# Routing of a two-block early-fusion network: the search for each expert's threshold, the ranking and the index rebuilt

## The reference

```
probs = softmax(x @ router_gate)                 # 3072 tokens, 8 experts
topw, topi = top_k(probs, 2);  topw /= topw.sum + 1e-9
gates[token, expert] = topw where chosen, else 0
top_g, tok_idx = top_k(gates.T, cap)             # cap = 960 tokens an expert
xe = x[tok_idx]
ye = (silu(xe @ gate_w) * (xe @ up_w)) @ down_w * top_g
out[tok_idx] += ye
```

## Time and profile before

| | |
|---|---|
| median of 3 runs | 2027.98 us (2025.38 to 2030.83) |
| profiled execution | 2033.92 us, its span 2032.1 us |
| PE, DVE, ACT, POOL busy | 1774.8, 1245.7, 973.9, 542.5 us |
| mean granted TensorE clock | 0.932 of full |
| PE in the chain that ended last | 70% |

### The profile page before, as it was taken

How to read it: one execution, slowest core, us unless ns; L and a number is a source line. 1 busy time by engine, 2 the same in 40 slices (tenths; PEclk the granted TensorE clock), 3 DMA queues, 4 the chain that set the end, 5 groups by cost and what they waited for, 6 DMA issues and landing times.

```text
span 2032.1 us, 35703 instructions
## 1 busy us (share of the span) xinstructions
PE 1774.8 (87%) x10949; PEld 1411.1 (69%) x10949; DVE 1245.7 (61%) x4049; ACT 973.9 (48%) x2658; POOL 542.5 (27%) x784
## 2 busy tenths in 40 slices
PE   3457999999999999899999999971369999999997
PEld 2245676767677676667777777751259989999896
DVE  6346686767768575856767677646745454445442
ACT  2025474665657566564666656630034353434431
POOL 2143334242433411111111111110052335333431
PEclk9568899999999999999999999985579999999999
DMA  6110101101010110102001110011032212212210
GB/s 188 48 34 17 50 2 57 34 24 58 0 42 0 55 32 1 32 1 79 6 31 31 31 31 23 16 61 29 0 119 90 81 47 95 76 53 69 73 38 20
DMA packets 74572, 90.20 MB, mean 44 GB/s; under 512 B 16539, under 2 KB 64710, under 8 KB 74472
## 3 DMA queue, kind: packets, MB, share of 16 engines
q1 hardware_dynamic: 65000, 72.32, 11.1%
q0 software_dynamic: 9472, 16.77, 2.9%
HBM read 71.09 MB, written 25.26 MB: 47 GB/s over the span
## 4 chain that ended last, share of the span: by engine, by line
PE 70%; issue 12%; DVE 8%; POOL 3%; DMA 2%; ACT 1%; DVEq 1%; POOLq 1%; SPq 1%; ACTq 0%
PE bank L1020 16%; PE bank L1490 16%; PE bank L1505 9%; PE bank L968 6%; PE bank L952 5%; PE bank L1003 5%; PE bank L891 2%; PE bank L1162 2%; PE bank L979 1%; PE bank L1042 1%; PE bank L876 1%; DVE probs L2120 1%; PE bank L892 1%; POOL rstd_a L2849 1%; PE bank L1475 1%
## 5 line engine op out<-in xcount | busy, mean ns | idle before, releaser
L1608 ACT ACTIVATE probs<-probs,nmax 128x128 f32<-128x128 f32 (+2 forms) x768 | 381.0, 501 | 75.0 <-DVE nmax L2120 74.8
L968 PE MATMUL bank<-cst,probs 128*128 128x128 f32 x1536 | 234.9, 279 | 19.5 <-ACT probsT L1616 11.8
L968 PEld LDWEIGHTS bank<-cst,probs 128*128 128x128 f32 x1536 | 182.8, 143 | 67.8 <-issue 25.4
L1490 PE MATMUL bank<-xeT,gate_w 128*128 128x480 f32 x768 | 187.1, 379 | 1.5 <-DVEq L2788 1.5
L1490 PE MATMUL bank<-xeT,up_w 128*128 128x480 f32 x768 | 186.9, 379 | 0.0
L2215 DVE COPY probsT<-bank 128x384 f32<-128x384 f32 x256 | 141.2, 552 | 72.1 <-PE bank L968 70.4
L1505 PE MATMUL bank<-down_w,hT 128*120 128x256 f32 x1536 | 182.8, 281 | 0.0
L1505 PEld LDWEIGHTS bank<-down_w,hT 128*120 128x120 f32 x1536 | 181.5, 182 | 0.1
L1616 ACT COPY probsT<-bank 128x384 f32<-128x384 f32 x256 | 121.9, 476 | 115.6 <-PE bank L968 107.0
L2891 POOL COPY rinv<-rowsum 128x384 f32<-128x384 f32 x80 | 40.8, 510 | 497.1 <-DVE o1T L2142 294.5
L2796 DVE TENSOR_TENSOR prod<-bank,sil 128x480 f32<-128x480 f32 x128 | 83.5, 656 | 146.3 <-PE bank L1490 146.3
(11 more groups left out here) (300 smaller groups left out, 3362.9 us busy)
## 6 DMA issues: line engine op xcount, KB each, us to landing
gate_raw<-in_L_ffn_gate_w SPq DMA_DIRECT2D x8, 1024.0 KB, 4.9
up_raw<-in_L_ffn_up_w SPq DMA_DIRECT2D x8, 1024.0 KB, 6.9
down_raw<-in_L_ffn_down_w SPq DMA_DIRECT2D x8, 1024.0 KB
img<-in_x SPq DMA_DIRECT2D x8, 768.0 KB, 5.5
residual_rows<-x SPq DMA_DIRECT2D x8, 384.0 KB, 2.5
residual_rows<-h_in SPq DMA_DIRECT2D x8, 384.0 KB, 3.8
xr<-residual_rows SPq DMA_DIRECT2D x8, 384.0 KB, 4.7
hr<-residual_rows SPq DMA_DIRECT2D x8, 384.0 KB, 3.9
```

The costliest lines, as they stand in the source:

```text
L968: last = tr(ps[bank][:, P * q:P * (q + 1)], probs[:, n % 4, SEG[t] + P * j:SEG[t] + P * (j + 1)], ident)
L1490: last = mm(ps[bank][:, 0:HALF], w[:, wp, c, P * m:P * (m + 1)], xeT[:, xp, c, HALF * hf:HALF * (hf + 1)], start=(c == 0 and k == 0), stop ...
L1608: last = f(p, p, ACT.Exp, bias=nmax[:, n % 4, t:t + 1], scale=-1.0, accum_out=rowsum[:, where, t:t + 1])
```

## The change

It has these parts:

1. **Output projection.** PE waits for the division of the pair before the last, sums seven of the eight products of each of the three tiles (in banks 0, 1 and 2, which stay open), and only then makes the last pair's values and turned divisors. The eighth products follow when the last pair is divided.
2. **Search on turned gates.** The gates of one expert (24 columns) are cut into two halves of 12; PE turns the two halves, so that 96 partitions (8 experts by 12) hold 256 tokens each. A candidate is then one number for each partition. A round is three scalar operations with an accumulated count, a product with a 96 x 96 matrix of "same expert", and four or five small operations. Its 15 rounds are written out, with the bits as constants. The threshold is turned back by PE.
3. **One ranking pass.** Ties and clear winners are summed, scanned and ranked in one pass of 384 columns.
4. **Index for expert 0 alone.** Its places are made from expert 0's column by itself (24 one-hot groups in three operations, 24 products), and its gather starts with `first_index`. The index for the others is made in the time of expert 0: one-hots on DVE (`others_hot`) before `hidden`, products on PE after the third pair of sums, the copy on DVE at the third step of `hidden`. Expert 0 is taken out of the loops of PE and DVE for that. The gather of expert 1 waits for this index.
5. **Weight split of expert 0.** ACT no longer waits for the index, and the lower part of the gate and up weights is made by POOL instead of DVE, before its wait for the index.

The core of the diff:

```
+            def rows_out(chunks):
+                for t in range(NT):
+                    ...
+                    for c in chunks:
+                        last = mm(ps[bank][:, 0:D], o1T[:, c, P * t:P * (t + 1)], wo1[:, c, :],
+                                  start=(c == 0), stop=(c == PAIRS - 1))
+            pe.wait_ge(freed[5], take0[5] + 2 * B + PAIRS * B - 1)
+            rows_out(range(PAIRS - 1))
             heads_out(1, PAIRS - 1, last_u)
             denominators_transposed(EPI, 0, "rinvT_tail", 1, last_u, PAIRS - 1)
             pe.wait_ge(freed[5], take0[5] + 2 * B + PAIRS * B)
-            for t in range(NT):
-                token_major(EPI, 0, "proj1", t, o1T, wo1, 8)
+            rows_out((PAIRS - 1,))
...
+            for r in range(SEARCH):
+                pe.wait_ge(counts_ready, r + 1)
+                mm(ps[7][0:GROUPS, 0:STEPS], const_cols("same_expert")[0:GROUPS, :], cnt[:], start=True, stop=True)
...
+            for name, left in (("totals", "ones"), ("earlier", "before")):
+                mm(ps[bank][:, 0:2 * E * TILES], const_cols(left), sel_eq[:].rearrange("p k n -> p (k n)"), ...
...
+            for n in range(TILES):
+                last = mm(ps[bank][0:CP, 0:CT], first_row[:, n, :], first_col[:, n, :], ...
...
+                    if q == 3 and aside is not None:
+                        aside()                      # PE: the 48 index products
...
+            gates(EXPERT, 0, 0, other_slots)
+            rows_transposed(EXPERT, 1, 0)
+            down(EXPERT, 0, 0)
+            with pe.Fori(1, E - 1) as e:
...
-            act.wait_ge(index_ready, 1)
             gate_uppers(0)
...
+            for r in range(SEARCH):
+                for q in range(STEPS):
+                    last = ts(at_least[:, q, :], by_group[:], as_gate[:, q:q + 1], 0.0, ALU.is_ge, ALU.add,
+                              accum_out=cnt[:, q:q + 1])
+                last.then_inc(counts_ready, 1)
+                if r > 0:
+                    tt(thr[:], thr[:], best[:], ALU.bitwise_or)
+                if r + 1 < SEARCH:
+                    then()
+                    tt(ahead[:], thr[:].to_broadcast([GROUPS, STEPS]), bits[:, r + 1, :], ALU.bitwise_or)
+                dve.wait_ge(counts_taken, r + 1)
+                stt(won[:], ps[7][0:GROUPS, 0:STEPS], float(CAP), bits[:, r, :], ALU.is_ge, ALU.mult)
+                then()
+                v.tensor_reduce(best[:], won[:], AX.X, ALU.max)
+                then()
+                if r + 1 < SEARCH:
+                    tt(cand[:], ahead[:], best[:].to_broadcast([GROUPS, STEPS]), ALU.bitwise_or)
...
+            v.tensor_copy(both(scan), k[:, 0:2 * E * TILES])
+            v.tensor_tensor_scan(both(earlier), const_cols("scan_keep"), both(scan), 0.0, ALU.mult, ALU.add)
...
+            tt(first_col[:], places(TILES, CT), spread(first_f[:, 1, :], CT), ALU.is_equal)
+            tt(first_row[:], places(TILES, CP), spread(first_f[:, 0, :], CP), ALU.is_equal)
+            tt(first_col[:], first_col[:].bitcast(F32), spread(token, CT), ALU.mult).then_inc(first_hot, 1)
...
+            def others_hot(g):
+                q, n = 8 * g, 8 * g % TILES
+                tt(col_hot[:, q:q + 8, :], places(8, E * CT), spread(col_f[:, q:q + 8], E * CT), ALU.is_equal)
+                tt(row_hot[:, q:q + 8, :], places(8, CP), spread(row_f[:, q:q + 8], CP), ALU.is_equal)
+                then()
+                tt(col_hot[:, q:q + 8, :], col_hot[:, q:q + 8, :].bitcast(F32), spread(token[:, n:n + 8], E * CT),
+                   ALU.mult).then_inc(hot_ready, 1)
...
-            gate_lowers(0)
             x_lowers(ROUTE, 0, 0)
+            for g in range(2 * TILES // 8):
+                others_hot(g)
+            down_lowers(0)
+            hidden(EXPERT, 0, 0, other_slots)
...
+            pool.wait_ge(gate_upper, 1)
+            for w, raw in ((gate_w, gate_raw), (up_w, up_raw)):
+                last = g.tensor_tensor(w[:, 1].rearrange("p c n -> p (c n)"), raw[:],
+                                       w[:, 0].rearrange("p c n -> p (c n)").bitcast(F32), ALU.subtract)
+            last.then_inc(gate_split, 1)
             pool.wait_ge(rows_cleared, 1)
             pool.wait_ge(gates_stored, 16)
-            pool.wait_ge(index_ready, 1)
+            pool.wait_ge(first_index, 1)
```

More of the change, by code:

```diff
@@ L472, in early_fusion_kernel @@
         (hT,), _ = region(end_e, ("hT", [P, 2, FM, CAP], F32R))
[L474 to L482, removed]
+        (pr, hots, gts, r_a, r_b, r_c), end_r = region(
+            end_e, ("pr", [P, E, TILES], F32), ("hots", [P, 2, E, TILES], F32),
+            *[(n, [P, E, TILES], F32) for n in ("gts", "r_a", "r_b", "r_c")])
@@ L1449, in _ @@
[L1449 to L1458, removed]
-            for q in range(2 * TILES):
-                if q % 8 == 0:
-                    pe.wait_ge(hot_ready, q // 8 + 1)
-                last = mm(ps[bank][0:CP, 0:E * CT], row_hot[:, q, :], col_hot[:, q, :],
-                          start=(q == 0), stop=(q == 2 * TILES - 1))
@@ L1464, in _ @@
-            last.then_inc(filled[bank], 1)
+                mm(ps[bank][:, 0:2 * E * TILES], const_cols(left), sel_eq[:].rearrange("p k n -> p (k n)"),
+                   start=True, stop=True).then_inc(filled[bank], 1)
+            pe.wait_ge(first_hot, 1)
+            bank = banks.bank(ROUTE, "first_index")
+            banks.wait_free(pe, ROUTE, "first_index")
+            for n in range(TILES):
+                last = mm(ps[bank][0:CP, 0:CT], first_row[:, n, :], first_col[:, n, :],
+                          start=(n == 0), stop=(n == TILES - 1))
@@ new lines, in _, with other_slots @@
+            last.then_inc(filled[bank], 1)
+            def other_slots():
+                bank = banks.bank(ROUTE, "index")
+                banks.wait_free(pe, ROUTE, "index")
+                for q in range(2 * TILES):
+                    if q % 8 == 0:
+                        pe.wait_ge(hot_ready, q // 8 + 1)
+                    last = mm(ps[bank][0:CP, 0:E * CT], row_hot[:, q, :], col_hot[:, q, :],
+                              start=(q == 0), stop=(q == 2 * TILES - 1))
+                last.then_inc(filled[bank], 1)
@@ L2719, in _ @@
             then()
-            tt(r_c[:], r_c[:], want[:].unsqueeze(2).to_broadcast([P, E, TILES]), ALU.is_lt)
+            k, f_ = bank_of(ROUTE, "earlier")
+            tt(both(earlier), both(scan), k[:, 0:2 * E * TILES], ALU.add).then_inc(f_, 1)
             then()
-            tt(r_c[:], r_c[:], eqm[:], ALU.mult)
+            ties_before, above_before = (earlier[:, z, :].rearrange("p (e n) -> p e n", e=E) for z in range(2))
+            left = want[:].unsqueeze(2).to_broadcast([P, E, TILES])
@@ L2729, in _ @@
             then()
[L2730 to L2741 removed]
+            stt(flat(r_c), flat(r_b), -float(NO_SLOT), flat(r_a), ALU.add, ALU.mult)
@@ new lines, in _ @@
+            tt(hot_code[:].rearrange("p k e n -> p k (e n)"), hots[:].rearrange("p k e n -> p k (e n)"),
+               flat(r_b).unsqueeze(1).to_broadcast([P, 2, E * TILES]), ALU.mult)
+            k, f_ = bank_of(ROUTE, "first_index")
+            ts(slot_token[0:CP, 0:CT], k[0:CP, 0:CT], float(NO_TOKEN), None, ALU.add).then_inc(f_, 1)
+            then()
+            v.nop().then_inc(first_index, 1)
+            for k in range(2):
+                v.tensor_reduce(kv[:, 6 + k, :], hot_code[:, k].rearrange("p e n -> p n e"), AX.X, ALU.add)
@@ L2742, in _ @@
+            then()
+            ts(code[:], kv[:, 6:8, :].rearrange("p k n -> p (k n)"), float(NO_SLOT), None, ALU.add)
             then()
@@ L2789, in x_lowers, with hidden @@
                 v.nop().then_inc(x_split, 2 * DC)
-            def hidden(section, e, i):
+            def hidden(section, e, i, aside=None):
                 for q in range(2 * FM + 1):
+                    if q == 2 and aside is not None:
+                        aside()
                     if q < 2 * FM:
```

199 lines of the change are left out of this document (107 added, 92 removed).

## The result

The changed kernel took 2008.17 us (median, 2007.8 to 2010.69) against 2029.4 for the kernel before in the same comparison: a ratio of 0.9896, interval 0.9871 to 0.9922, so 21.2 us less. 2010 was forecast, 17.7 us less. Run again later it gave 2011.81 against 2029.41, ratio 0.9917 (0.9901 to 0.9932). Its profiled execution took 2010.69, span 2008.9.

A forecast was written before the change was run, and what follows sets the result against it. A 149.2 us chain of dependent steps from the last attention values to expert 0's first product was taken as the bound. +1.8 +0.3 -9.7 +1.0 +6.5 -21.0 -5.6 +9.0 = -17.7 us gave a 2010 us median, range 1997 to 2021.

The forecast's parts named there:

- Projection, +1.8: Output projection: 21 of 24 products early fill no idle gap and queue DVE's three tiles; 1.8 us later, bounds 0 and +3.
- Search, -8.7 with fetches: Threshold search: fifteen rounds of 2.8 us gain 9.7, less 1.0 guessed for fetches of unrolled code.
- POOL's split, +6.5 (way in +0.3): Search's start: POOL's weight split holds DVE's two-input SBUF operations, 6.5 us; extra steps before the first scan, 0.3.
- From the last threshold to the gather, -21.0: Ranking and expert 0's index: 42.2 us become 21.2, bounds 18 and 25.
- The gather, -5.6: First gather to expert 0's first product: 21.4 us become 15.8, without DVE's split and expert 1's weights beside it.
- The alternative of -14.8 in all: Expert 0's gather: by the skill page DVE's two-input operations don't hold POOL's DMA issues, so 2.9 us of gain stays away.
- Expert 0, +9.0: Expert 0: one-hots and index products delay up3 until DVE returns bank 7, 8.3 us, plus 0.7 for the clock.
- (a): Search's start: POOL's split holds nothing on DVE; 2003.5 us, chance 0.16.
- (b): Search: POOL's split holds nothing and rounds take 2.3 us; 1996 us, chance 0.07.
- (d): Search: POOL's split, far slower than extrapolated, becomes its bound; at four times the price 2039 us, chance 0.03.
- (e): Whole change does little: search rounds 3.2 us, lock 9.5, tail 25; 2023 us, chance 0.04.
- (c): Expert 0: PE at half clock through the mixed stretch loses 18 us instead of 9; 2019 us, chance 0.12.

The follow-up runs named there:

- the two undoings: Changed kernel with all 24 output projection products late again: ratio 0.9875; kernel before with only the early projection products: 1.0009. Both against the kernel before.
- a2: Changed kernel with expert 0's weight split moved from POOL to DVE's wait for the 24 index products: 2000.66 us, ratio 0.9838 to the kernel before.
- a4: Changed kernel with the weight split made by DVE beside the gather of expert 0's rows, as before the change: ratio 0.987 to the kernel before.
- a7: Changed kernel with POOL's weight split held back until the search is over, so beside the ranking: ratio 0.9852 to the kernel before.
- a5: Changed kernel with three of six one-hot groups made while DVE waits for expert 0's rows: ratio 0.9885 to the kernel before.
- a9: Changed kernel with late projection, DVE's split in the index-product wait, and the others' index spread over the gather: 1989.77 us, ratio 0.9813 to the kernel before.

## Why the prediction was right, point by point

The stretches sum to -20.4 where -17.7 was forecast. Two misses of opposite sign lie in this: the search gained 4.7 more than forecast, the way into it and the router lost 3.0 more (2.1 and 0.9). That the sum is nearer than its terms is luck.

**Projection, +1.8: right in this profile** (+1.9; +1.7 and +1.9 by the two undoings), and in its parts: PE's last product came 0.6 later (forecast 0.35), and from there to the last normalisation it was 3.68 instead of 2.31, DVE's queue of three tiles (forecast 3.7). Its lower bound, 0 with the clock up, is the case too: +0.2 in four of nine profiles. Which of the two a profile shows is chance. Missed: the router's products, behind 2.96 us of idle PE instead of 1.59, come at half clock, 0.9 more in this stretch.

**Search, -8.7 with fetches: right in kind, too small** (-13.4). Three scans took 1.28 from first start to last end, where I had 1.3. Mis-sized was the turn through PE, "0.72 kept": 0.57, the pair of records is 0.48 long for 96 rows and 3 columns instead of 0.62 for 128 and 24. That is 2.2 us in 15 rounds. The three small steps were 0.71 together instead of 0.78, 1.1 us in 15 rounds. And the 1.0 for fetches was not there.

**POOL's split, +6.5 (way in +0.3): right in mechanism, 2 us too small** (+8.9 together; 8.6 of it is the split, a2). POOL's price was 4.50 and 4.60 against 4.75, so 2.2 ns a column where the two rows give 2.5. The place was wrong: I held `ahead` and `cand` of the first round and gave DVE the steps between as progress. In fact the addition `gts` was held first, then the copy of the first candidates, which has one input; DVE advanced by nearly nothing under either. I hadn't asked whether a copy of three columns can be held.

**From the last threshold to the gather, -21.0: right** (-21.6); nearly every piece is within 0.1. The terms given for the wide sum (0.06, four times 0.32, 0.4) make 1.74 and not the 1.65 that was used; 1.69 was measured. The 0.4 for fetch stalls was not there.

**The gather, -5.6: right** (-5.3), and its cause is shown: a4 brings 4.2 back with DVE's split alone. The alternative of -14.8 in all, by which a two-input operation of DVE wouldn't hold the gathers, falls with it.

**Expert 0, +9.0: right** (+8.3), and the wait that ends last is the one forecast: up3 behind DVE's copy out of bank 7, at 19.2 us after the first product (forecast 19.7), with the one-hots done at 14.7 (forecast 15). Off was PE's own path to that point. I had gate3 done at 17.3 and PE waiting 2 us and more; gate3 came at half clock and ended at about 19, so PE was held for only about 0.2 us in this profile (its weight load for 0.7) and for 1.27 in a7. So PE's path is nearly as long as DVE's, and taking DVE's work away (a5) leaves 6.7 of the loss. What is lost behind up3, 0.7 for the clock in the forecast, was 0.5 in this profile and up to 2.6 in the others.

Of the rivals, (a), and (b) with it, falls by DVE's 4.65 us beside POOL's 4.50, and (d) by the 4.50 itself; (e) wanted rounds of 3.2, which were 2.56; (c) had the half clock in expert 0 but not its size. (The range was said to go from (b) and began at 1997, where (b) gives 1996.) Not settled is the scatter of the mark ahead of the change, 12 us over thirteen profiles of the same code, and what sets the clock in a given execution.

## What to carry to other kernels

Work given to POOL does not run beside DVE's if DVE has operations with two inputs in SBUF there, or, as here, a copy from SBUF to SBUF: look for DVE's idle time first, and if POOL must do it, cut it into short instructions. In a chain of waits, work moved into a busy engine's time costs its own length: PE's 48 small products cost five microseconds in expert 0, while 32 of them in the gather's gaps cost next to nothing (17.55 in a9 against 17.46 in a5). Where two engines' paths into a wait are nearly equal, shortening the one that ends last gives back only their difference, here 1.6 us. Summing early pays only if it fills an idle time; ask which event the new wait is for, and what used to overlap with the old order.

## What was not expected of the hardware

A DVE copy of 96 x 3 integers took 4.44 us beside a POOL subtraction of 4.60. A run of PE products with 64 moving columns, 5.13 us without a gap and with PE busy for all of the 8 us ahead, was followed by a clock of 0.50; behind the 16 of a9 it stayed up. POOL's subtractions of 2048 columns in eight pieces took 5.83 and 5.49 us instead of 4.50 and 4.60, so a piece costs 0.11 to 0.17 more than its share. Six experts took 65.58 us each in every one of thirteen profiles, while expert 0, with the index products in it, took 76.1 to 78.1 in eight profiles of the same code.
